# A four-stage transformer block: who splits weights, copies rows and writes results in its two expert loops

## The chip, the cores and the metric

One core of one Trainium2 chip runs the whole program. The metric is the device time of one execution in microseconds; the median of 3 runs of the kernel before is 1306.93 us (1305.28 to 1307.9).

## The reference, cut to what matters

Four stages on x of shape (4, 512, 256), each with a layer norm in front and a gated residual behind: a local AFT attention with its feed-forward, a mixture of experts (8 experts, 2 chosen for each token, squared relu, 256 hidden columns) beside a shared feed-forward, a slot attention with a GRU (3 iterations), and a second mixture of experts (8 experts, 2 chosen, silu gate, 512 hidden columns, biases).

```
x = x + tanh(g_xattn[0]) * L0_xattn(layernorm(x), ctx)
x = x + tanh(g_ffn[0])   * L0_ffn(layernorm(x))      # first expert loop, m = 0
x = x + tanh(g_xattn[1]) * L1_xattn(layernorm(x), ctx)
x = x + tanh(g_ffn[1])   * L1_ffn(layernorm(x))      # second expert loop, m = 1
# L0_ffn:  y = square(relu(x @ w1[e].T)) @ w2[e].T   for the two experts e of a token, weighted
# L1_ffn:  y = (silu(x @ gate[e] + b) * (x @ up[e] + c)) @ down[e] + d
```

## The kernel before

The kernel is written by hand for the five sequencers (TensorE, VectorE, ScalarE, GpSimd, and SP, which only issues DMAs); each works off its own program in order and waits on semaphores. Batches n = 0..3 go in two pairs (h = 0, 1). Part A makes the first attention, the shared feed-forward and the routing; part C makes slot attention and the second routing. The orders of the work there are lists of stages, one for each engine. Layer norms take the reciprocal root from GpSimd (`power`, line 836), the first of them right after GpSimd's constants.

Routing scatters each normalised token, with its place of return appended as 8 columns, into the HBM array `routed[m]`, sorted by expert (`scatter`, line 843, indirect DMAs of GpSimd). A table (lines 680 to 717) tells where each group of G = 256 rows lies and which groups each expert has: here 19 groups in the first loop and 21 in the second. `fill` (line 458) writes blank rows behind the last row of each expert: three of the fills go before the first group is fetched, five behind the first two.

The expert loops (`moe_sp`, `moe_pool`, `moe_act`, `moe_dve`, `moe_pe`) run for both m. The outer loop over experts is unrolled, the inner one over an expert's groups has its bounds from the table (`bounds`, lines 399 and 400, two register loads for each engine and expert). All products are made in three parts from a high (float32r) and a low part (the rest) of each operand: `product`, lines 210 to 212. A group t goes like this:

- SP fetches the rows of group t + 2 into `xg` (line 451, after TensorE has turned the rows of the group before) and their places into `places` (line 452).
- TensorE makes the up products of group t, then transposes the rows of group t + 1 (line 640), then waits for y of the group before and for the low part of h (`hlo`), and makes the down products into PS[5] and PS[6].
- ScalarE: relu (562), square into the high part of h (564), for each of the two blocks f of 128 hidden columns; then the high part of the next rows (544).
- VectorE: product for h in PSUM for each block (599), low part of h (588), low part of the next rows (581); then, when the down products are ready, for each half a: wait until the last write of this half has landed (`yout`), copy the places of this expert (620), copy y from PSUM to SBUF (622; in the second loop with the bias DB added, 624).
- GpSimd waits for each half of y and writes its 128 rows to `results[m]` at their places (535).

Weights of an expert come twice: `raw_in` (line 429) loads them as they are, from ScalarE's queue in the first loop, from SP's in the second; `weights_hi` (line 498) loads them once more with a cast DMA of GpSimd straight into the high part; `weights_lo` (line 507) subtracts on GpSimd (the very first of the second loop on VectorE). Weights of expert e + 2 are fetched during expert e. Between them ScalarE's queue also fetches the weights of part C (`attention_weights`, line 437), whose WHH has its high part by a cast DMA of GpSimd.

`y_free` (line 517) writes two blank rows into `results[m]`, so that `yout` counts have a start: for m = 0 after the last scatter, for m = 1 after the first loop. DB, the bias rows of the second loop's down product spread over 128 partitions (1 MB), is loaded by SP before the second routing ends (line 792).

## Time and profile before

| | us |
|---|---|
| median of 3 runs | 1306.93 |
| the profiled execution | 1311.5, its span 1309.7 |
| TensorE busy in the span | 1122.4 (86%) |
| VectorE, ScalarE, GpSimd busy | 738.5, 384.2, 375.3 |
| first expert loop, from the first up products to the last down products | 353.93 to 477.62 (start of the last product) |
| second expert loop, from the first up products to the first half of the last y | 1071.15 to 1281.2 |

The profile is of one execution. A row of its timeline has the start and the length of an instruction (of several in a row, where it ends with x2 and more), the engine, the line of the kernel, what is written and read, and in brackets how long the engine had been idle before it and what released it. "q" behind an engine is its sequencer, where DMAs are issued and registers are loaded. Matmuls overlap: a 128x256 product is listed with 0.28 us, and a new one starts every 0.12 us at the full clock of TensorE and every 0.21 us at half of it.

### The profile page before, as it was taken

What the parts mean: (1) busy time and instruction counts of PE and PEld (TensorE: products, weight loads), DVE (VectorE), ACT (ScalarE), POOL (GpSimd) and SP (SyncE); (2) the same over time, 40 slices, a digit from 0 to 9 for tenths busy, and PEclk for the clock granted to TensorE, in tenths of its full rate; (3) what the DMA queues carried; (4) which work ended last, traced back from release to release, by engine and by line L of the source; (5) the groups of instructions that cost most, each with busy time, mean ns of one, the idle gap of its engine ahead of it and who ended that gap; (6) DMA issues with size and microseconds to landing.
All of it is one profiled execution on the core that took longest, in us unless ns stands there. A gap on an engine that the chain in (4) does not pass through costs nothing.

```text
span 1309.7 us, 17730 instructions
## 1 busy us (share of the span) xinstructions
PE 1122.4 (86%) x5875; PEld 884.8 (68%) x5875; DVE 738.5 (56%) x1888; ACT 384.2 (29%) x705; POOL 375.3 (29%) x312
## 2 busy tenths in 40 slices
PE   7999899898767577899999977999999749999991
PEld 5568575685656454676887835787878439998990
DVE  5576736767344435555655554445453746666664
ACT  3131230313133224234243333243332123333330
POOL 2423161322444540001111133010101464544710
PEclk8999999999898878999999989999999969999996
DMA  9001060000566643000000000000000586555416
GB/s 324 1 0 33 3 202 8 1 1 17 160 189 181 207 127 105 22 1 1 1 1 2 1 33 34 1 1 1 1 1 1 162 259 204 153 148 169 129 56 209
DMA packets 90852, 102.93 MB, mean 79 GB/s; under 512 B 18336, under 2 KB 75936, under 8 KB 90656
## 3 DMA queue, kind: packets, MB, share of 16 engines
q1 hardware_dynamic: 65920, 59.85, 15.1%
q0 software_dynamic: 20240, 36.72, 9.1%
q10 hardware_dynamic: 4624, 5.51, 1.2%
q8 instruction: 37, 0.61, 0.2%
q14 instruction: 31, 0.25, 0.1%
HBM read 73.31 MB, written 28.74 MB: 78 GB/s over the span
## 4 chain that ended last, share of the span: by engine, by line
PE 47%; DVE 16%; another core or an unknown queue 11%; issue 7%; DMA 6%; ACT 5%; POOL 4%; SPq 3%; DVEq 1%; POOLq 0%; ACTq 0%
PE PS L210 11%; PE PS L212 10%; PE PS L211 10%; PE PS L1710 6%; PE PS L1600 2%; POOL routed L843 2%; PE PS L1572 2%; DMA results<-y,place_of 2%; POOL rstd L836 1%; DMA split<-down_w 1%; DVE SM L1397 1%; DVE hs L588 1%; PE PS L1628 1%; DMA places<-routed 1%
## 5 line engine op out<-in xcount | busy, mean ns | idle before, releaser
L836 POOL TENSOR_TENSOR rstd<-ve,minus_half 128x4 f32<-128x4 f32 x40 | 40.5, 1013 | 359.9 <-DVE ve L1099 215.0
L535 POOL DMA_INDIRECT results<-y,place_of x80 | 78.2, 978 | 186.6 <-DVE y L624 110.4
L1484 PE MATMUL PS<-ones_bf 128*128 128x512 bf16 x393 | 105.8, 417 | 16.6 <-DMA routed<-S,dest 13.5
L210 PE MATMUL PS<-xt,split 128*128 128x256 f32 x312 | 90.8, 291 | 9.3 <-issue 6.2
L1710 PE MATMUL PS<-VP,HB 128*128 128x257 f32 x384 | 85.8, 382 | 4.4 <-DVE VP L1410 4.4
L211 PE MATMUL PS<-xt,split 128*128 128x256 f32 x312 | 89.5, 287 | 0.0
L212 PE MATMUL PS<-xt,split 128*128 128x256 f32 x312 | 89.4, 287 | 0.0
L1484 PEld LDWEIGHTS PS<-ones_bf 128*128 128x128 bf16 x393 | 39.7, 107 | 70.4 <-issue 39.4
L843 POOL DMA_INDIRECT routed<-S,dest x64 | 66.8, 1044 | 67.0 <-DVE dest L1179 49.5
L1710 PEld LDWEIGHTS PS<-VP,HB 128*128 128x128 f32 x384 | 72.5, 190 | 17.4 <-DVE VP L1410 7.3
L210 PE MATMUL PS<-split,hs 128*128 128x256 f32 x184 | 59.5, 324 | 24.1 <-DVE hs L588 23.2
L567 ACT ACTIVATE act<-PS,colv 128x256 f32<-128x256 f32 x84 | 39.8, 474 | 121.9 <-PE PS L212 114.1
L210 PEld LDWEIGHTS PS<-xt,split 128*128 128x128 f32 x312 | 61.2, 196 | 11.6 <-issue 8.0
L603 DVE SCALAR_TENSOR_TENSOR act<-PS,colv,act 128x256 f32<-128x256 f32 x84 | 40.6, 484 | 37.8 <-ACT act L567 29.6
L210 PE MATMUL PS<-HTS,WHH 128*128 128x512 f32 x144 | 60.5, 420 | 1.5 <-DVE RT L1115 1.5
L211 PEld LDWEIGHTS PS<-xt,split 128*128 128x128 f32 x312 | 61.2, 196 | 0.0
L212 PEld LDWEIGHTS PS<-xt,split 128*128 128x128 f32 x312 | 61.1, 196 | 0.0
L1039 ACT ACTIVATE HB<-PS,SM 128x512 f32<-128x512 f32 x48 | 33.0, 687 | 94.0 <-DVE SM L1399 93.6
L1572 PE MATMUL PS<-EWT,HB 128*128 128x512 f32 x128 | 57.4, 608 | 3.0 <-DVE EWT L1238 3.0
L210 PEld LDWEIGHTS PS<-split,hs 128*128 128x128 f32 x184 | 36.6, 199 | 32.4 <-issue 25.8
L210 PE MATMUL PS<-RT,WIH 128*128 128x512 f32 x144 | 57.2, 397 | 0.0
L212 PE MATMUL PS<-RT,WIH 128*128 128x512 f32 x144 | 56.9, 395 | 0.0
(339 smaller groups left out, 2970.7 us busy)
## 6 DMA issues: line engine op xcount, KB each, us to landing
xg<-routed SPq DMA_DIRECT2D x42, 256.0 KB
HB<-results SPq DMA_DIRECT2D x16, 512.0 KB, 5.8
routed<-blank SPq DMA_DIRECT2D x20, 264.0 KB, 6.8
raw<-gate_w SPq DMA_DIRECT2D x8, 512.0 KB
raw<-up_w SPq DMA_DIRECT2D x8, 512.0 KB
raw<-down_w SPq DMA_DIRECT2D x8, 512.0 KB
split<-m_w POOLq DMA_DIRECT2D x12, 256.0 KB, 3.3
split<-gate_w POOLq DMA_DIRECT2D x6, 512.0 KB
```

The source lines that it names most:

```text
L210: pe.matmul(out_, a[1], b[0], start=first, stop=False)
L211: pe.matmul(out_, a[0], b[1], start=False, stop=False)
L212: return pe.matmul(out_, a[0], b[0], start=False, stop=last)
L535: pool.indirect_dma_start(out=results[m], out_offset=bass.IndirectOffsetOnAxis(ap=place_of[:, a:a + 1], axis=0), in_=w.y[:, a], in_offset= ...
L567: act.activation(w.act[:, f % 2, 0], PS[:, f, 0:G], ACT.Sigmoid, bias=col("gate_b", b)).then_inc(sem(f"m{m}_act"), 1)
L603: dve.scalar_tensor_tensor(out=a[:, 1], in0=PS[:, f, 0:G], scalar=col("gate_b", e * w.fc + f), in1=a[:, 0], op0=ALU.add, op1=ALU.mult).the ...
L836: pool.tensor_tensor(rstd[h][:], ve[h][:], minus_half[:], ALU.pow).then_inc(sem("rstd_ready"), 1)
L843: pool.indirect_dma_start(out=routed[m], out_offset=bass.IndirectOffsetOnAxis(ap=dest[m][:, n, j, kk:kk + 1], axis=0), in_=S2T[h][:, j], i ...
L1039: act.activation(HB[h][:, j], bank(h, j), ACT.Exp, bias=SM[h][:, 1, j:j + 1], scale=1.0 / 16, accum_out=SM[h][:, 2, j:j + 1]).then_inc(sem ...
L1484: pe.matmul(free.rearrange("p (a b) -> p a b", b=P), ones_bf[:], ones_bf[:].unsqueeze(1).to_broadcast([P, TT, P]), start=True, stop=True)
L1572: ins = pe.matmul(bank(h, b + c), w[:, j, c * P:(c + 1) * P], EWT[:, j], start=j == 0, stop=j == TT - 1)
L1710: ins = pe.matmul(bank(h, j)[:, 0:D + 1], HB[h][:, m, j * P:(j + 1) * P], VP[h][:, m, 0:D + 1], start=m == 0, stop=m == TT - 1)
```

## The change

- y of the first loop is copied by one instruction of ScalarE for both halves, behind the high part of the next rows; VectorE only copies the places, one instruction for both halves. There are two buffers of y and of places, for even and odd groups, and VectorE waits for the landing of the group before the last.
- GpSimd's loop for m = 0 has no experts and no weights any more: it takes two groups in a body, one with each buffer, and a last group behind. The high parts of the weights of the first loop are made by ScalarE (experts 2 to 7) and the low parts by VectorE, at the start of the expert before; on the first pair GpSimd copies the high parts of experts 0 and 1 instead of loading them. In the second loop ScalarE makes the high parts of experts 0 and 1, the others stay cast DMAs.
- The places travel with the rows: `group_in` fetches all 264 columns with one DMA, `xg` is a piece of the buffer S2T[0], and VectorE copies the 8 columns into `tags` (`tag`) between its last product and its first low part, after TensorE has turned them. SP fetches the next rows after `tagged`, not after `turned`. SP's loop has no experts either; before its third group it waits for all fills.
- `raw_in` of the second loop moves from SP's queue to ScalarE's, the two loads of X move from SP at expert 5 to ScalarE at expert 7, and the high part of WHH is made by ScalarE after the first loop.
- `y_free` for both loops moves to the start of GpSimd's program, ahead of its first `power`; for m = 0 the second half has three DMAs, and the second and third wait for the landing of the one before.
- DB is loaded after `first_group_in(sp, 1)`; VectorE waits for it (`cw_raw`, 96) after the first `x_lo` of the second loop.

```diff
-        places = sb("places", [P, (NG + 2) * (G // P), E])
-        place_of = sb("place_of", [P, G // P], I32)
+        tags = sb("tags", [P, 2, G // P, E])
+        place_of = sb("place_of", [P, 2, G // P], I32)
...
-            w.xg = sb(f"xg{m}", [P, G // P, D], F32, st)
+            w.xg = S2T[0][:, 0:G // P]
             w.xt = sb(f"xt{m}", [P, 2, C, G], F32R, st)
             w.act = sb(f"act{m}", [P, 2, w.ups, G], F32, st)
             w.hs = sb(f"hs{m}", [P, 2, w.fc, G], F32R, st)
-            w.y = sb(f"y{m}", [P, G // P, D], F32, st)
+            w.y = S1[1][:].rearrange("p (i a) d -> p i a d", i=2)
...
-        first_rows = S1[0][:, 0:G // P]
+        first_rows = S2T[0][:, G // P:2 * (G // P)]
         def group_in(sp, m, t):
             r = sp.value_load(table[m][0:1, bass.ds(t + 2 * E, 1)], min_val=0, max_val=XROWS - G)
             if not isinstance(t, int):
                 counted(sp, m)
-                sp.wait_ge(sem(f"m{m}_turned"), t)
-            into, name = (first_rows, "first_rows") if isinstance(t, int) and t == 0 else (moe[m].xg[:], f"m{m}_xg")
-            sp.dma_start(into, routed[m][bass.ds(r, G), 0:D].rearrange("(a p) d -> p a d", p=P)).then_inc(sem(name), 16)
-            sp.dma_start(places[:, bass.ds(t * (G // P), G // P)], routed[m][bass.ds(r, G), D:D + E].rearrange("(a p) e -> p a e", p=P))\
-              .then_inc(sem(f"m{m}_places"), 16)
+                sp.wait_ge(sem(f"m{m}_tagged"), t)
+            into, name = (first_rows, "first_rows") if isinstance(t, int) and t == 0 else (moe[m].xg, f"m{m}_xg")
+            sp.dma_start(into, routed[m][bass.ds(r, G), :].rearrange("(a p) d -> p a d", p=P)).then_inc(sem(name), 16)
...
+        def all_groups(eng, m):
+            return eng.value_load(table[m][0:1, 2 * E - 1:2 * E], min_val=E, max_val=NG)
         def moe_sp(sp, m):
-            for e in range(E):
-                if e == 1:
-                    sp.wait_ge(sem("filled"), 16 * (4 + (m + 1) * (E - 3)))
-                if m == 1 and e + 2 < E:
-                    raw_in(sp, m, e + 2)
-                if m == 0 and e == 5:
-                    for n, h in of_pair[0]:
-                        sp.wait_ge(sem(f"x_out{h}"), 16 * PAIRS)
-                        sp.dma_start(X[h][:], x_base[0, n].rearrange("(j p) d -> p j d", p=P)).then_inc(sem(f"x_in{h}"), 16)
-                lo, hi = bounds(sp, m, e)
-                with sp.Fori(lo, hi) as t:
-                    group_in(sp, m, t + 2)
-            moe_end(sp, m, hi)
-        def weights_hi(pool, m, e):
-            w = moe[m]
+            sp.wait_ge(sem("filled"), 16 * (4 + (m + 1) * (E - 3)))
+            total = all_groups(sp, m)
+            with sp.Fori(2, total + 1) as t:
+                group_in(sp, m, t)
+            moe_end(sp, m, total)
...
+        def weights_cast(pool, e):
+            w = moe[1]
             if e >= 3:
-                done = pool.value_load(table[m][0:1, e - 2:e - 1], min_val=1, max_val=NG - 1)
-                counted(pool, m)
-                pool.wait_ge(sem(f"m{m}_down"), done)
-            for ap, at, n in expert_sources(m, e):
-                pool.dma_start(w.split[e % 3][0][:, at:at + n].rearrange("p (c o) -> p c o", c=ap.shape[1]), ap).then_inc(sem(f"m{m}_hi{e % 2}"), 16)
+                done = pool.value_load(table[1][0:1, e - 2:e - 1], min_val=1, max_val=NG - 1)
+                counted(pool, 1)
+                pool.wait_ge(sem("m1_down"), done)
+            for ap, at, n in expert_sources(1, e):
+                pool.dma_start(w.split[e % 3][0][:, at:at + n].rearrange("p (c o) -> p c o", c=ap.shape[1]), ap).then_inc(sem(f"m1_cast{e % 2}"), 16)
+        def raw_there(eng, m, e):
+            eng.wait_ge(sem(f"m{m}_raw{e % 2}"), 16 * (m + 2) * (e // 2 + 1))
+        def weights_hi(eng, m, e):
+            raw_there(eng, m, e)
+            hi = moe[m].split[e % 3][0]
+            if eng is nc.scalar:
+                eng.activation(hi, raw_of(m, e), ACT.Copy).then_inc(sem(f"m{m}_hi"), 1)
+            else:
+                eng.tensor_copy(hi, raw_of(m, e)).then_inc(sem(f"m{m}_hi"), 1)
         def weights_lo(eng, m, e):
-            w = moe[m]
-            k = len(list(expert_sources(m, e)))
-            eng.wait_ge(sem(f"m{m}_hi{e % 2}"), 16 * k * (e // 2 + 1))
-            eng.wait_ge(sem(f"m{m}_raw{e % 2}"), 16 * k * (e // 2 + 1))
-            hi, lo = w.split[e % 3]
+            raw_there(eng, m, e)
+            if m == 0 or e < 2:
+                eng.wait_ge(sem(f"m{m}_hi"), e + 1)
+            else:
+                eng.wait_ge(sem(f"m1_cast{e % 2}"), 16 * 3 * (e // 2))
+            hi, lo = moe[m].split[e % 3]
             eng.tensor_tensor(lo, raw_of(m, e), hi.bitcast(F32), ALU.subtract).then_inc(sem(f"m{m}_lo"), 1)
...
         def y_free(pool, m):
             for a in range(G // P):
-                pool.dma_start(results[m][2 * B * T + a:2 * B * T + a + 1], blank[0:1, a, 0:D]).then_inc(sem(f"m{m}_yout{a}"), 16)
-        def moe_pool(pool, m):
-            w = moe[m]
-            pool.wait_ge(sem(f"m{m}_table"), 1)
+                for k in range(1 if m else 1 + 2 * a):
+                    if k:
+                        pool.wait_ge(sem(f"m{m}_yout{a}"), 16 * k)
+                    pool.dma_start(results[m][2 * B * T + 2 * k + a:2 * B * T + 2 * k + a + 1], blank[0:1, a, 0:D]).then_inc(sem(f"m{m}_yout{a}"), 16)
+        def rows_out(pool, m, i, a, name):
+            pool.indirect_dma_start(out=results[m], out_offset=bass.IndirectOffsetOnAxis(ap=place_of[:, i, a:a + 1], axis=0),
+                                    in_=moe[m].y[:, i, a], in_offset=None).then_inc(sem(name), 16)
+        def moe_pool_first(pool):
+            pool.wait_ge(sem("m0_table"), 1)
+            total = all_groups(pool, 0)
+            def group_out(t, i):
+                counted(pool, 0)
+                pool.wait_ge(sem("m0_y"), t + 2)
+                pool.sem_inc(sem("passed"), 1)
+                for a in range(G // P):
+                    rows_out(pool, 0, i, a, f"m0_yout{i}")
+            with pool.Fori(0, total // 2) as k:
+                for i in two:
+                    group_out(2 * k + i, i)
+            group_out(total - 1, 0)
+            moe_end(pool, 0, total)
...
-                if m == 0 and e + 2 < E:
-                    raw_in(act, 0, e + 2)
+                if e + 2 < E:
+                    raw_in(act, m, e + 2)
                 if m == 0 and 2 <= e < 7:
                     attention_weights(act, e - 2)
+                elif m == 0 and e == 7:
+                    for n, h in of_pair[0]:
+                        act.dma_start(X[h][:], x_base[0, n].rearrange("(j p) d -> p j d", p=P)).then_inc(sem(f"x_in{h}"), 16)
+                if m == 0 and 2 <= e + 1 < E:
+                    weights_hi(act, 0, e + 1)
...
                         h_hi(t, w.fc - 1)
+                    else:
+                        act.wait_ge(sem("m0_placed"), t + 1)
+                        act.wait_ge(sem("m0_down"), t + 1)
+                        act.activation(w.y[:, bass.ds(t % 2, 1)].rearrange("p i a d -> p (i a) d"), PS[:, 5:7, 0:D], ACT.Copy).then_inc(sem("m0_y"), 1)
             if m == 0:
                 moe_end(act, m, hi)
         def moe_dve(dve, m):
             w = moe[m]
+            def tag(n):
+                dve.wait_ge(sem(f"m{m}_turned"), n)
+                rows = first_rows if isinstance(n, int) else w.xg
+                dve.tensor_copy(tags[:, bass.ds((n - 1) % 2, 1)], rows[:, :, D:D + E].unsqueeze(1)).then_inc(sem(f"m{m}_tagged"), 1)
             def x_lo(n):
                 dve.wait_ge(sem(f"m{m}_xhi"), n)
...
+            tag(1)
             x_lo(1)
+            if m == 1:
+                dve.wait_ge(sem("cw_raw"), 96)
             for e in range(E):
+                if m == 0 and 2 <= e + 1 < E:
+                    weights_lo(dve, 0, e + 1)
...
+                        if f == w.fc - 1:
+                            tag(t + 2)
...
-                    dve.wait_ge(sem(f"m{m}_down"), t + 1)
-                    dve.wait_ge(sem(f"m{m}_places"), 16 * t + 16)
-                    for a in range(G // P):
-                        dve.wait_ge(sem(f"m{m}_yout{a}"), 16 * t + 16)
-                        dve.tensor_copy(place_of[:, a:a + 1], places[:, bass.ds(t * (G // P) + a, 1), e])
-                        if m == 0:
-                            dve.tensor_copy(w.y[:, a], PS[:, 5 + a, 0:D]).then_inc(sem(f"m{m}_y"), 1)
-                        else:
-                            dve.tensor_tensor(w.y[:, a], PS[:, 5 + a, 0:D], DB[:, e], ALU.add).then_inc(sem(f"m{m}_y"), 1)
+                    if m == 0:
+                        dve.wait_ge(sem("m0_yout0"), 32 * (t // 2) + 16)
+                        dve.wait_ge(sem("m0_yout1"), 32 * ((t + 1) // 2) + 16)
+                        dve.tensor_copy(place_of[:, bass.ds(t % 2, 1)], tags[:, bass.ds(t % 2, 1), :, e]).then_inc(sem("m0_placed"), 1)
+                    else:
+                        dve.wait_ge(sem("m1_down"), t + 1)
+                        for a in range(G // P):
+                            dve.wait_ge(sem(f"m1_yout{a}"), 16 * t + 16)
+                            dve.tensor_copy(place_of[:, 0, a:a + 1], tags[:, bass.ds(t % 2, 1), a, e])
+                            dve.tensor_tensor(w.y[:, 0, a], PS[:, 5 + a, 0:D], DB[:, e], ALU.add).then_inc(sem("m1_y"), 1)
...
-            sp.dma_start(DB[:], down_b.rearrange("e d -> (e d)").partition_broadcast(P).rearrange("p (e d) -> p e d", d=D)).then_inc(sem("db_in"), 16)
             first_group_in(sp, 1)
+            sp.dma_start(DB[:], down_b.rearrange("e d -> (e d)").partition_broadcast(P).rearrange("p (e d) -> p e d", d=D)).then_inc(sem("cw_raw"), 16)
...
+            pool.wait_ge(sem("blank"), 2)
+            for m in two:
+                y_free(pool, m)
...
-            pool.wait_ge(sem("blank"), 2)
-            y_free(pool, 0)
             pool.wait_ge(sem("batch_a"), B)
-            moe_pool(pool, 0)
-            y_free(pool, 1)
-            pool.wait_ge(sem("cw_hi"), 16)
+            moe_pool_first(pool)
+            pool.wait_ge(sem("cw_hi"), 1)
...
-                    if n == B - 1:
-                        pool.wait_ge(sem("batch_c"), B)
-                        for e in range(2):
-                            weights_hi(pool, 1, e)
...
+            act.wait_ge(sem("cw_raw"), 80)
+            act.activation(WHH[:, 0], raw_whh, ACT.Copy).then_inc(sem("cw_hi"), 1)
...
+            for e in range(2):
+                weights_hi(act, 1, e)
...
-            dve.wait_ge(sem("db_in"), 16)
```

## Rows read from the trace of the kernel before

**Rows 1.** One row for each stretch: us, busy us (count) of PE, PEld, DVE, ACT, POOL
```profile
353.00:479.00 126.00, 81.44 (x532) 75.75 (x532) 56.87 (x170) 38.24 (x96) 57.92 (x53) 0.87 0.63 181
...
1066.00:1290.00 224.00, 205.29 (x1608) 194.17 (x1606) 140.67 (x358) 78.86 (x192) 100.03 (x67) 0.98 0.50 148
```

**Rows 2.** Timeline, one group of the first loop: ScalarE, VectorE, TensorE
```profile
381.49 0.36 ACT L562 ACTIVATE act<-PS 128x256 f32<-128x256 f32 x1
...
382.81 0.74 DVE L588 TENSOR_TENSOR hs<-PS,hs 128x256 fp32r<-128x256 f32 x2
...
383.37 0.36 PE L210 MATMUL PS<-split,hs 128*128 128x256 f32 x1 [1.51 <-DVE hs L588]
```

**Rows 3.** Timeline, TensorE, first down product of a later group
```profile
420.79 0.36 PE L210 MATMUL PS<-split,hs 128*128 128x256 f32 x1 [0.92 <-DVE hs L588]
```

**Rows 4.** Timeline, TensorE and VectorE where the expert changes
```profile
384.76 0.28 PE L212 MATMUL PS<-split,hs 128*128 128x256 f32 x1
...
388.04 0.15 DVE L620 CAST place_of<-places 128x1 int32 x1 [1.17 <-DMA results<-y,place_of]
...
388.11 0.41 DVE L622 COPY y<-PS 128x256 f32<-128x256 f32 x1
...
389.69 0.43 DVE L599 SCALAR_TENSOR_TENSOR PS<-PS,act 128x256 f32<-128x256 f32 x1 [1.16 <-issue]
...
390.92 0.55 PE L210 MATMUL PS<-RT,hs 128*128 128x256 f32 x1 [3.25 <-DVE hs L588]
```

**Rows 5.** Timeline, TensorE, the longest wait at a change of expert
```profile
443.38 0.55 PE L210 MATMUL PS<-RT,hs 128*128 128x256 f32 x1 [5.21 <-DVE hs L588]
```

**Rows 6.** Timeline, ScalarE's DMA issues, and two instructions on 128x1024 of other stages
```profile
382.13 0.41 ACTq L429 DMA_DIRECT2D raw<-m_w  x1
...
383.16 0.61 ACTq L437 DMA_DIRECT2D HB<-Wv  x1
...
1033.04 1.02 ACT L936 ACTIVATE RT<-PS 128x1024 fp32r<-128x1024 f32 x1 [0.60 <-PE PS L1478]
...
11.52 1.23 DVE L1193 TENSOR_TENSOR EMB<-EMB,S 128x1024 f32<-128x1024 f32 x1
```

**Rows 7.** Timeline, TensorE, the rows of the third group and the down products behind
```profile
366.35 1.12 PE L640 MATMUL PS<-ident,xg 128*128 128x128 f32 x4 [4.64 <-DMA xg<-routed]
...
367.12 0.56 PE L210 MATMUL PS<-split,hs 128*128 128x256 f32 x1
```

**Rows 8.** Timeline, GpSimd at the start; line 517; issues to landing; chain; line 535
```profile
2.76 0.29 POOL L826 TENSOR_SCALAR_AFFINE_SELECT tri<-ones_bf 128x128 bf16<-128x128 bf16 x1
...
9.03 1.04 POOL L836 TENSOR_TENSOR rstd<-ve,minus_half 128x4 f32<-128x4 f32 x1 [5.97 <-DVE ve L1099]
...
L517 POOL DMA_DIRECT2D results<-blank x4: 520/540/560, 341.8 to 484.3; - x4
...
results<-blank POOLq DMA_DIRECT2D x2, 1.0 KB, 5.8
...
420.66 3.44 DMA places<-routed
...
DMA to landing us min/median/max: 2.4/2.4/4.3
```

**Rows 9.** Timeline, SP and VectorE at the second loop; issues to landing at the start
```profile
1035.25 2.79 SPq L792 DMA_DIRECT2D DB<-down_b  x1
...
1069.63 5.70 SPq L458 DMA_DIRECT2D routed<-blank  x5
...
1073.41 0.49 DVE L603 SCALAR_TENSOR_TENSOR act<-PS,colv,act 128x256 f32<-128x256 f32 x1 [2.31 <-ACT act L567]
...
band<-pos_bias SPq DMA_DIRECT2D x1, 1024.0 KB, 8.4
...
W<-w SPq DMA_DIRECT2D x1, 1024.0 KB, 11.3
```

**Rows 10.** Timeline, GpSimd's next instruction behind the first pair's weights
```profile
235.79 1.04 POOL L836 TENSOR_TENSOR rstd<-ve,minus_half 128x4 f32<-128x4 f32 x1 [32.96 <-DVE ve L1099]
```

38 lines of the change are left out of this document (17 added, 21 removed).

## The prediction

> **What bounds the kernel now.** The program is one TensorE stream with a few places where TensorE waits for others, so I read by stretch and not by share of the whole span. First the stretches of the two expert loops: in the first TensorE is busy 81 of 126 us, in the second 205 of 224 [rows 1]. So the second loop is TensorE's own, and whatever delays its first group is paid in full; the first loop loses 45 us to waits. Then the timeline of one group in the first loop, to see which wait it is. The reader is to see the chain: relu of the second hidden block on ScalarE at 381.49, VectorE's low part of the first block at 382.81, the down products at 383.37 after a wait of 1.51 us [rows 2]. VectorE's two product instructions and, ahead of them, its copies of y are what lies between. Where those copies are early, the same wait is 0.92 us [rows 3]. Last, the group at which the expert changes: VectorE stands still until the results' write has landed, then copies y at 388.11, then loads the loop bounds and restarts at 389.69, and the down products wait 3.25 us [rows 4]. There are seven such changes. Their waits are 1.51, 3.25, 3.58, 3.55, 5.21, 4.35 and 1.87 us, 23.3 us together (the second in [rows 4], the longest in [rows 5]). Of the ten other groups from the fourth on, two wait 1.5 to 1.6 us and eight 0.7 to 1.1 us (one of each in [rows 2, 3]).
>
> **First loop, inside an expert.** Removed from VectorE: two y copies of 0.41 us and two index copies of 0.15 us [rows 4]. They are on the path in two groups: 1.2 us gained (1.51 less 0.92, twice). Added: the tag copy, small like an index copy, between the second product and the first low part, where every group has it; its issue hides under the product, so I take 0.1 us, 1.1 us for eleven groups. If it hid nothing it would be 0.15 us, if all, 0. The y copy goes to ScalarE as one 128x512 instruction between the down products and the next relu. The next relu has to wait for the new group's first up products anyway, six of the twelve, which are nearly as long as the copy, so I take 0.1 us a group, 1.1 us; with no overlap it would be 0.6 us a group, with a full one 0. What is late next is again the relu, square, relu chain. ScalarE's wait for `down` queues its own relu behind it, and nobody else's work.
>
> **First loop, the change of expert.** Removed: the wait for the landed write (two buffers now), GpSimd's cast DMAs and its subtraction. Added on ScalarE, behind the last y copy: two or three DMA issues of 0.4 to 0.6 us, then the high part of 128x1024, 1.02 us like its equal [rows 6]. Added on VectorE: the low part, 1.23 us like its equal [rows 6], which waits for ScalarE, and behind which the bounds and the first product are queued. From the last down product (end 385.04, [rows 4]): y copy issued +0.3; three DMA issues, 1.65, +1.95; high part done +3.0; VectorE starts the low part, and with bounds loaded during it (388.11 to 389.69, 1.58 us, is that load beside a copy, [rows 4]) the first product starts +4.6, the second +4.95, tag, low part of h +5.35, down products +5.9. TensorE has ended its transposes at +2.6 (390.92 less 3.25, less 385.04). So the wait is 3.3 us in the five changes with a third DMA, 2.7 in the first, and about 2.5 in the last, which has no weights but two loads of X: 21.7 us for 23.3. The long waits for a landed write go, and ScalarE's and VectorE's new work takes their place: 1.6 us gained. Bounds: if none of the new work were on the path, all seven would be like the two short ones (1.7 us), 11 us gained; if the high part and the bounds of ScalarE lay one behind the other, 5 us lost.
>
> **First loop, third group.** Its rows keep TensorE waiting for 4.64 us, until 366.35 [rows 7]. SP fetched them late, after five fills and two writes of x_base. SP now waits for all fills before that fetch, and has two transfers and one bounds load fewer: about even, within 1.5 us either way. The down products of the second group, which started at 367.12, halfway through the transposes [rows 7], now wait for the end of these (367.47), the tag and the low part behind it: 368.2, 1.1 us lost. Sum of the loop: -1.2 + 1.1 + 1.1 - 1.6 + 1.1 = +0.5 us, from -12 to +6.
>
> **Start of the kernel.** `y_free` is moved ahead of GpSimd's first `power`, with six DMAs for four, and between three of them it waits for the landing. GpSimd is free at 3.05 and its `power` starts at 9.03, released by VectorE; VectorE, TensorE and all else of the first pair wait for it [rows 8]. Each issue is 0.54 us [rows 8]. With L the time from issue to landing, GpSimd is free at 3.05 + 0.54 + 2L + 3 x 0.54 = 5.2 + 2L. Two rows bound L: the same one-row DMA, sent while the other queues were filling the engines, took 5.8 us, and a small transfer amid weight loads 3.44 us [rows 8]. Here all 16 engines are loading inputs, so I take the middle, 4.6: free at 14.4, and the kernel is 5.4 us late from its first layer norm on. Nothing absorbs it: inputs are there by then. Ends: L of 2.4, the shortest landing of the indirect writes [rows 8], gives +1.0; 5.8 gives +7.8.
> The Trainium skill (DMA: Bandwidth & Descriptors, Anatomy of one DMA) fits a DMA from GpSimd as 2.0 us plus its bytes; by that alone this edit would cost 0.2 us, 5 less than my sum. It also says that an engine goes round its queues in turn. The 5.8 us for one row [rows 8] speak against taking the fit for a loaded machine, so I stay with the rows.
>
> **Start of the second loop.** DB, 1 MB, was loaded at 1035.25; its issue alone takes 2.79 us. It now goes behind the eight fills and two row fetches. The five late fills start at 1069.63 and take 5.70 us [rows 9]; two place transfers fewer make that 1.2 us earlier, so DB's issue starts at about 1074.2. Transfers of the same size in a loaded stretch land 8.4 to 11.3 us after issue [rows 9]; weights and fills load this stretch as well. I take 8.4: 1082.6. VectorE waits for it after its first x_lo, and the bounds and all products of group 0 are queued behind: 1.3 us more, 1083.9 where it was 1073.41 [rows 9]. TensorE, with the up products done, waits for the low parts. VectorE's work per block is its pace before, so the delay reaches the down products whole: +10.5 us, and [rows 1] leave no slack to win it back. Ends: landing 5 us after issue (its own issue and the shortest landing), +7.1; 11.3 us, +13.4. The cover that this load had was the whole routing of the last batches; it is gone.
>
> **What costs nothing.** On the first pair GpSimd makes the high parts by copying instead of cast DMAs, up to 1.3 us later at the second; it then stands idle 33 us [rows 10]. High part of WHH on ScalarE: 1.5 us by the 1.02 for 1024 columns [rows 6], under the eight transposes that TensorE does there; without them it would cost that. High parts of the second loop's first two experts on ScalarE fall where it idles before the table; the raw loads issued by ScalarE in the second loop lie in its wait for the up products. X is fetched 30 us later than before, still a whole expert before use. Writing results from two buffers ends as before, two issues and a landing after the last y.
>
> **Sum.** 0.5 + 5.4 + 10.5 = +16.4 us on the profiled execution's 1311.5 us (span 1309.7), which itself is 4.6 above the median 1306.93. The differences are carried over to the median: 1323.
>
> **Rivals.** (a) Faster: the boundary work of ScalarE and VectorE overlaps fully and TensorE, waiting less, also keeps its full clock; the loop gains 12 us from the waits and some 8 from clock. With head +1.0 and DB +7.1 that is 1295. For it: waits of 5.21 and 4.35 us do vanish [rows 5]. Against: the low part needs the high part, and that needs ScalarE's turn. Chance 0.11. (b) Even: the loop gains 12, the head costs 1 and DB 10.5: 1306.5, within noise. Chance 0.07. (c) Slower still, by one mechanism: at each change of expert ScalarE's DMA issues, high part and bounds load go one after another and TensorE idles beyond 4 us, falling to half clock for the next group; six times 2 us, decisive once the wait passes that of [rows 4]: 1323 + 12 = 1335. Chance 0.16. (d) The forecast, both waits real: 1323, 1312 to 1332. Chance 0.66.
>
> **How the numbers follow.** A difference of 0.2%, 2.6 us, is what a measurement of this kernel can tell from none. Faster: (a), 0.11, and a hundredth of (d). Same: (b), 0.07. Slower: the rest, 0.81. The range goes from 1307, above (a) and most of (b), to 1335, the place of (c).
>
> **What would show it.** GpSimd's first power at about 14.4 with landings of results<-blank before it; in the second loop VectorE's first product at about 1084 plus the shift, waiting for DB, and TensorE idle 8 us or more before its first down products. In the first loop: waits of 2.5 to 3.3 us at all changes, none above 4, ended by VectorE, and VectorE's low part released by ScalarE. I am wrong if DB lands before VectorE has made x_lo, if the power starts before 10, or if the stretch of the first loop, 126 us in [rows 1], is not within 114 to 132.

## The result, and the profile of the changed kernel

| | before | after |
|---|---|---|
| median of the runs, us | 1307.41 (1305.28 to 1313.71, 4 runs) | 1364.47 (1362.91 to 1365.28, 4 runs) |
| profiled execution, us (its span) | 1311.5 (1309.7) | 1362.91 (1361.2) |
| mean granted clock of TensorE | 0.947 | 0.934 |

The change makes the kernel 4.3% slower: ratio 1.0433, interval 1.0407 to 1.0459, 57 us where 16 were forecast. The spans of the two profiled executions differ by 51.5 us only: that of before took 4.1 us more than its median, that of the change 1.6 less. Read from TensorE's instructions in both traces:

| stretch of TensorE | before, us | after, us | difference |
|---|---|---|---|
| start to the first up products of the first loop | 353.93 | 363.82 | +9.9 |
| to the last down products of the first loop | 122.3 | 116.4 | -6.0 |
| to the first up products of the second loop | 594.9 | 592.0 | -2.9 |
| to its first down products | 6.2 | 18.9 | +12.7 |
| to its last down products | 199.4 | 237.9 | +38.5 |

The busy time of each engine in the two loops (columns: the stretch and its length, then busy us and instructions of TensorE, its weight loads, VectorE, ScalarE, GpSimd, then granted clock, DMA share, GB/s), to be read against [rows 1]:

```profile
363.00:486.00 123.00, 81.78 (x532) 75.19 (x532) 51.34 (x140) 55.36 (x121) 36.65 (x38) 0.87 0.49 151
1072.00:1342.00 270.00, 214.47 (x1596) 206.34 (x1596) 167.62 (x379) 78.59 (x191) 94.18 (x65) 0.90 0.39 121
```

In the second loop TensorE is busy 9 us more than in [rows 1], at a clock of 0.90 for 0.98, and idle 37 us more. VectorE is busy 27 us more, with work that hardly changed: that is the first sign, for an instruction's time as the profile counts it includes the time in which it is held up. The costliest forms of VectorE's copies of the tags show which instruction it is (count, busy us, mean ns, idle time before it), and the line's own view its spread (shortest, median, longest, ns):

```profile
L618 DVE COPY tags<-S 128x16 f32 x40 | 34.1, 852 | 1.7 <-issue 1.7
L618 DVE COPY tags<-S x42: 163/166/6435, 362.5 to 1330.2; 128x16 f32 x40, 128x16 f32<-128x16 f32 x2
```

The median is 0.166 us and the longest 6.4 us. The timelines of VectorE, GpSimd and TensorE at the third group (start us, us, engine, line, operation; the time idle before it and its releaser in brackets):

```profile
1114.11 6.43 DVE L618 COPY tags<-S 128x16 f32 x1
1120.46 0.41 DVE L629 TENSOR_TENSOR hs<-PS,hs 128x256 fp32r<-128x256 f32 x1
...
1113.78 6.73 POOL L517 TENSOR_TENSOR third_split<-raw,third_split 128x3072 fp32r<-128x3072 f32 x1
...
1120.92 0.58 PE L210 MATMUL PS<-split,hs 128*128 128x256 f32 x1 [6.42 <-DVE hs L629]
```

GpSimd's subtraction starts at 1113.78 and ends at 1120.51; VectorE's copy of 16 columns starts a third of a us later and ends at 1120.54. The low part of h stands behind it, and TensorE stops in the midst of its down products for 6.42 us and comes back slower (0.58 us, then 0.41 to 0.42 each, for instructions that took 0.28 before the stop). It happens six times: at 1114.11, 1152.67, 1188.09, 1234.22, 1260.34 and 1286.84, with copies of 6.43, 4.58, 4.66, 4.68, 4.63 and 2.44 us. The six sets of down products take 10.6, 8.8, 8.9, 8.9, 8.9 and 6.3 us where the others take 3.4: 32 of the 38.5 us. Cut the other way, from the first down products to the last, TensorE is idle for 34.8 us where before has 7.5, and busy for 203.1 where before has 191.9, at a granted clock of 0.93 for 1.00: 27 us more of waiting and 11 us more of running at the lower clock after the stops.

The start of the kernel, GpSimd and below it VectorE, against [rows 8]:

```profile
3.37 1.25 POOL L525 DMA_DIRECT2D results<-blank  x2 [0.31 <-POOL tri L875]
9.79 0.48 POOL L525 DMA_DIRECT2D results<-blank  x1 [5.18 <-DMA results<-blank]
14.66 1.43 POOL L525 DMA_DIRECT2D results<-blank  x3 [4.39 <-DMA results<-blank]
16.11 1.07 POOL L888 TENSOR_TENSOR rstd<-ve,minus_half 128x4 f32<-128x4 f32 x1
17.14 1.93 POOL L901 TENSOR_SCALAR_AFFINE_SELECT band<-band 128x2048 f32<-128x2048 f32 x1
...
17.22 4.63 DVE L1159 TENSOR_SCALAR EMB<-X,mv,rstd 128x256 f32<-128x256 f32 x4 [8.81 <-POOL rstd L888]
```

The two waits for landings put `power` at 16.11, 7.1 us late, and VectorE's scaling, released by it, then runs beside GpSimd's two selects on `band` (the position bias, of which they keep a band) and takes 4.63 us where before it took 1.38. Together that is the 10 us of the table.

The start of the second loop, on SP, on the chain of waits (start us, us, what) and on VectorE, against [rows 9]:

```profile
1068.79 6.09 SPq L457 DMA_DIRECT2D routed<-blank  x5
1074.91 0.47 SPq L842 DMA_DIRECT2D DB<-down_b  x1
...
1074.91 12.29 DMA DB<-down_b
1087.24 0.32 DVEq L399
...
1088.71 0.48 DVE L649 SCALAR_TENSOR_TENSOR act<-PS,colv,act 128x256 f32<-128x256 f32 x1 [16.63 <-issue]
```

DB lands 12.29 us after its issue; bounds (L399, L400) and the first product stand behind the wait, and the first down products start at 1091.01 after 11.10 us of idle TensorE.

The first loop, at the second change of expert, on ScalarE, VectorE and TensorE, against [rows 4] and [rows 6]:

```profile
396.99 0.60 ACT L608 ACTIVATE S<-PS 128x512 f32 x1 [1.90 <-PE PS L212]
397.15 0.90 ACTq L429 DMA_DIRECT2D raw<-m_w  x2
398.14 0.43 ACTq L437 DMA_DIRECT2D HB<-Wv  x1
398.62 1.06 ACT L505 ACTIVATE split<-S 128x1024 fp32r<-128x1024 f32 x1 [1.03 <-issue]
...
399.78 1.22 DVE L517 TENSOR_TENSOR split<-S,split 128x1024 fp32r<-128x1024 f32 x1 [3.68 <-ACT split L505]
401.23 0.77 DVE L645 SCALAR_TENSOR_TENSOR PS<-PS,act 128x256 f32<-128x256 f32 x2 [0.23 <-issue]
...
402.45 0.38 PE L210 MATMUL PS<-RT,hs 128*128 128x256 f32 x1 [3.16 <-DVE hs L629]
```

That is the forecast chain: ScalarE's y copy, its three issues, the high part, VectorE's low part and products, the down products. The waits at the seven changes are 3.85, 3.16, 3.17, 3.02, 3.59, 2.09 and 2.14 us, 21.0 together.

### The profile page after: what moved, and what is told of

Same layout as the page of the kernel before. It is cut to its first block, busy times and chain, and to the rows that moved or that the text cites. A ratio compares the mean times of both kernels' runs of the same rounds, so it can differ in the third digit from the quotient of the medians.

```text
span 1361.2 us, 17338 instructions
## 1 busy us (share of the span) xinstructions
PE 1127.6 (83%) x5875; PEld 893.9 (66%) x5875; DVE 763.4 (56%) x1879; ACT 408.6 (30%) x733; POOL 345.3 (25%) x287
## 3 DMA queue, kind: packets, MB, share of 16 engines
q1 hardware_dynamic: 45920, 48.82, 11.3%
## 4 chain that ended last, share of the span: by engine, by line
PE 48%; DVE 17%; another core or an unknown queue 11%; issue 8%; ACT 5%; POOL 4%; DMA 3%; SPq 1%; ACTq 1%; DVEq 1%; POOLq 0%
PE PS L210 12%; PE PS L212 11%; PE PS L211 10%; PE PS L1757 6%; POOL routed L895 2%; PE PS L1647 2%; PE PS L1619 2%; POOL rstd L888 1%; DVE hs L629 1%; DVE SM L1445 1%; DVE act L649 1%; PE PS L1525 1%; ACT HB L1085 1%; DMA DB<-down_b 1%
## 5 line engine op out<-in xcount | busy, mean ns | idle before, releaser
L528 POOL DMA_INDIRECT results<-S,place_of x80 | 77.7, 971 | 267.8 <-DVE S L673 154.7
L210 PE MATMUL PS<-split,hs 128*128 128x256 f32 x184 | 62.5, 340 | 53.1 <-DVE hs L629 50.0
L210 PE MATMUL PS<-xt,split 128*128 128x256 f32 x312 | 93.7, 300 | 8.9 <-issue 5.9
L211 PE MATMUL PS<-xt,split 128*128 128x256 f32 x312 | 91.9, 295 | 0.0
L212 PE MATMUL PS<-xt,split 128*128 128x256 f32 x312 | 91.6, 294 | 0.0
L210 PEld LDWEIGHTS PS<-xt,split 128*128 128x128 f32 x312 | 64.2, 206 | 11.7 <-issue 7.9
L211 PEld LDWEIGHTS PS<-xt,split 128*128 128x128 f32 x312 | 64.2, 206 | 0.0
L212 PEld LDWEIGHTS PS<-xt,split 128*128 128x128 f32 x312 | 63.6, 204 | 0.0
```

Of the source, the lines that this page charges most:

```text
L210: pe.matmul(out_, a[1], b[0], start=first, stop=False)
L211: pe.matmul(out_, a[0], b[1], start=False, stop=False)
L212: return pe.matmul(out_, a[0], b[0], start=False, stop=last)
L528: pool.indirect_dma_start(out=results[m], out_offset=bass.IndirectOffsetOnAxis(ap=place_of[:, i, a:a + 1], axis=0), in_=moe[m].y[:, i, a], ...
```

## The experiments

Two theories at the outset. **Lock**: GpSimd and VectorE share a way to SBUF that one instruction holds to its end, and a VectorE copy or scaling from SBUF to SBUF needs it. **Rival**: the long copies wait for something of their own (the row that they read, their data type, descriptor writing by GpSimd's queue). Beside them stand DB's place in SP's queue and `y_free`'s place in GpSimd's as causes of their own. Each time is given as the ratio to the kernel before, measured beside it; a difference to the changed kernel is that of the two ratios times 1307. It carries about 4 to 6 us of uncertainty, an estimate from the 95% intervals of the ratios. In the expectations e1 is kernel 1 below, and so on.

**1. The tag copy on ScalarE.** Behind `x_hi`, in both loops; VectorE waits for it only ahead of the place copy. In the second loop ScalarE first waits for y of the group before.

```diff
                     x_hi(t + 2)
                     if m == 1:
+                        act.wait_ge(sem("m1_y"), 2 * t + 1)
+                    tag(t + 2)
+                    if m == 1:
                         h_hi(t, w.fc - 1)
...
-                        if f == w.fc - 1:
-                            tag(t + 2)
...
+                    dve.wait_ge(sem(f"m{m}_tagged"), t + 1)
```

> The changed kernel with the tag copy on ScalarE in both loops (behind the high part of the next rows) and VectorE waiting for it only before it copies the places. In the changed kernel six tag copies of the second loop, beside GpSimd's subtraction of weights, last 2.8 to 6.4 us instead of 0.17 us, and the low part of h is queued behind them. Theory P (the copy from SBUF to SBUF and GpSimd's subtraction cannot run at once): no long tag copy is left, because ScalarE does not share with GpSimd; all down products of the second loop from its second group on take 3.4 us; 1364 minus 32 to 38 us, so 1326 to 1332. Rival W (what is late there are the weights or rows, because the loads moved from SP's queue to ScalarE's, and the copy only shows it): the down products of those six groups stay 5 to 7 us too long and the time stays within 4 us of 1364.

Measured: 1330.9 us, ratio 1.0179 (1.0156 to 1.0203), 33 us less than the change. GpSimd, ScalarE, and the first and the last of TensorE's down products of one group:

```profile
1141.14 6.88 POOL L517 TENSOR_TENSOR split<-raw,split 128x3072 fp32r<-128x3072 f32 x1
...
1142.96 0.23 ACT L575 ACTIVATE tags<-S 128x16 f32 x1
...
1142.00 0.36 PE L210 MATMUL PS<-third_split,hs 128*128 128x256 f32 x1
...
1145.37 0.28 PE L212 MATMUL PS<-third_split,hs 128*128 128x256 f32 x1
```

The subtraction still takes 6.9 us, ScalarE's copy in the midst of it 0.23, and the down products are back at 3.4. VectorE's products and low parts, of which at least one input lies in PSUM, run through beside the subtraction at their usual 0.41 to 0.49 us. That rules out late weights or rows, the rival in the expectation. The tag copy carries the greater part of the loss; the run doesn't say yet what holds it.

**2. DB ahead of the fills again.**

```diff
+            sp.dma_start(DB[:], down_b...).then_inc(sem("cw_raw"), 16)
             first_group_in(sp, 1)
-            sp.dma_start(DB[:], down_b...).then_inc(sem("cw_raw"), 16)
```

> The changed kernel with the load of DB back ahead of first_group_in of the second loop. Theory D (VectorE waits for DB, which lands 12.3 us after its issue at 1074.91): VectorE's first product of the second loop starts about 1.5 us after x_lo as before, TensorE does not wait 11.1 us ahead of its first down products; 12 to 14 us less, so 1350 to 1352. If the first group is late for another reason (fills, rows, table load of ScalarE), the time stays within 3 us of 1364 and that wait stays above 8 us.

Measured: 1352.93 us, ratio 1.0338 (1.0318 to 1.0358), 12.4 us less than the change by the ratios and 11.5 by the medians. DB's issue stands at 1043.03, and TensorE's first down products at 1083.56 directly behind the transposes, with no wait. The term is real: TensorE's wait of 11.10 us, and 1.6 us by which the first two sets of down products are longer behind it (4.9 and 3.4 us from first to last start, here 3.9 and 2.8).

**3. `y_free` behind the second `power`.**

```diff
-            pool.wait_ge(sem("blank"), 2)
-            for m in two:
-                y_free(pool, m)
...
             power(1)
+            pool.wait_ge(sem("blank"), 2)
+            for m in two:
+                y_free(pool, m)
```

> The changed kernel with both y_free behind GpSimd's second power, where it is idle for some 20 us. Theory Y (the two waits for a landing, 5.2 us each, hold GpSimd's first power, and the band selection behind it holds VectorE's scaling, 4.63 us instead of 1.38 us): the first power is at about 9.0 us, VectorE's scaling takes 1.4 us, its second statistics are at 17.0 us instead of 27.4; 10 us less, so 1353 to 1356. If the band load or another input were the bound anyway, VectorE's second statistics would stay behind 20 us and no more than 4 us would come back.

Measured: 1354.69 us, ratio 1.0371 (1.0337 to 1.0404), 8.1 us less by the ratios, 9.8 by the medians; the first up products stand at 354.26 for 363.82. `power` is back at 8.56 and, what matters for experiment 6, the band select now comes after the scaling:

```profile
8.56 1.04 POOL L885 TENSOR_TENSOR rstd<-ve,minus_half 128x4 f32<-128x4 f32 x1 [5.51 <-DVE ve L1147]
14.35 1.92 POOL L898 TENSOR_SCALAR_AFFINE_SELECT band<-band 128x2048 f32<-128x2048 f32 x1 [4.74 <-DMA band<-pos_bias]
...
9.64 1.38 DVE L1159 TENSOR_SCALAR EMB<-X,mv,rstd 128x256 f32<-128x256 f32 x4 [1.23 <-POOL rstd L885]
```

The select waits for its own load until 14.35; only because `y_free` pushed `power` beyond that do the two meet.

**4. GpSimd's subtraction in two halves.**

```diff
+            if m == 1 and e >= 2:
+                k = moe[m].cols // 2
+                eng.tensor_tensor(lo[:, 0:k], raw_of(m, e)[:, 0:k], hi[:, 0:k].bitcast(F32), ALU.subtract)
+                eng.tensor_tensor(lo[:, k:], raw_of(m, e)[:, k:], hi[:, k:].bitcast(F32), ALU.subtract)...
```

> The changed kernel with GpSimd's subtraction for experts 1 to 7 of the second loop made as two instructions on 1536 columns each instead of one on 3072 (from expert 2 on). Theory P with a lock held for one whole instruction: the tag copy waits only for the rest of the first half; the six long copies (about 5 us each) shrink to 1.5 to 3.4 us or vanish, and 12 to 25 us come back: 1340 to 1352. If VectorE had to wait until GpSimd has nothing queued that reads SBUF, the copies stay as long and so does the time, within 3 us of 1364. Rival W: no change either, but then the copies' length has no relation to the end of a half.

Measured: 1366.97 us, ratio 1.0455 (1.043 to 1.048): no gain. GpSimd and VectorE:

```profile
1115.96 3.49 POOL L519 TENSOR_TENSOR third_split<-raw,third_split 128x1536 fp32r<-128x1536 f32 x1
1119.37 3.46 POOL L520 TENSOR_TENSOR third_split<-raw,third_split 128x1536 fp32r<-128x1536 f32 x1
...
1116.29 6.58 DVE L623 COPY tags<-S 128x16 f32 x1
```

The copy waits through both halves. The second half begins (1119.37) before the record of the first ends (1119.45), and VectorE isn't let in between. All six long copies are like that. But two GpSimd instructions in line don't always count as one. At the start of the changed kernel GpSimd's second select waits by semaphore for its first, and there VectorE's first two scalings end one behind each select (GpSimd's second select; VectorE's first and second scaling):

```profile
19.14 1.92 POOL L904 TENSOR_SCALAR_AFFINE_SELECT band<-band 128x2048 f32<-128x2048 f32 x1
...
17.22 2.02 DVE L1159 TENSOR_SCALAR EMB<-X,mv,rstd 128x256 f32<-128x256 f32 x1 [8.81 <-POOL rstd L888]
...
19.15 2.05 DVE L1159 TENSOR_SCALAR EMB<-X,mv,rstd 128x256 f32<-128x256 f32 x1
```

The first select ends at 19.07, the first scaling at 19.24. So VectorE waits as long as GpSimd's instructions stand back to back, and got its turn where GpSimd had waited in between. Halves with a wait between them weren't tried.

**5. Tags as integers.** The copy becomes a cast from fp32 to int32 of the same 128x16.

```diff
-        tags = sb("tags", [P, 2, G // P, E])
+        tags = sb("tags", [P, 2, G // P, E], I32)
```

> The changed kernel with the tags kept as int32, so that VectorE's tag copy turns float32 into int32 on its way; engine, place and size (128x16) stay. What is open: whether the form of the instruction or only its source in SBUF makes it wait for GpSimd. In the kernel before, VectorE's cast of 128x1 from SBUF ran in 0.15 us while GpSimd's subtraction ran. Theory F (only the plain copy has to wait): no long tag copy, 32 to 38 us less than 1364, 1326 to 1332. Theory S (a wide enough read from SBUF waits in either form): the six long copies and 1364 stay.

Measured: 1367.6 us, ratio 1.046 (1.0443 to 1.0476). The cast waits like the copy:

```profile
1116.90 6.46 DVE L618 CAST tags<-S 128x16 f32 x1
...
1116.59 6.73 POOL L517 TENSOR_TENSOR third_split<-raw,third_split 128x3072 fp32r<-128x3072 f32 x1
```

So the form of the output isn't it. One form is exempt, though, and it is the one from which I had priced the tag copy. In the kernel before, ten place copies of 128x1 fall inside GpSimd's subtractions, and none takes over 0.15 us (GpSimd, then VectorE, of before):

```profile
1097.05 6.88 POOL L507 TENSOR_TENSOR third_split<-raw,third_split 128x3072 fp32r<-128x3072 f32 x1
...
1102.39 0.15 DVE L620 CAST place_of<-places 128x1 int32 x1 [1.77 <-DMA places<-routed]
```

Experiment 1 has the same: casts of 128x1 inside the subtractions take 0.15 us. 128x1 isn't held and 128x16 is, as copy and as cast. Where between them the border lies, and whether it is the count of columns or the layout, wasn't tried.

**6. The band select behind the first scaling.** GpSimd's select waits until VectorE has finished its first embedding.

```diff
             pool.wait_ge(sem("pb_in"), 16)
+            pool.wait_ge(sem("emb"), 1)
```

> The changed kernel, y_free in front as it is, but GpSimd's selection on the band waits until VectorE has made the first EMB. Theory: of the 10 us at the start, 3.2 us are VectorE's scaling (SBUF to SBUF, 4.63 us for 1.38 us) standing still while GpSimd selects; with the hold it takes 1.4 us, nothing waits for the band, and 3 us come back: about 1361. If the scaling is slow for the DMA traffic, it stays at 4.6 us and so does the time.

Measured: 1364.15 us, ratio 1.0439 (1.0423 to 1.0454): no gain in the total. In the trace the mechanism is there (VectorE, then GpSimd):

```profile
17.30 1.38 DVE L1160 TENSOR_SCALAR EMB<-X,mv,rstd 128x256 f32<-128x256 f32 x4 [8.63 <-POOL rstd L888]
...
19.86 1.75 DVE L1248 TENSOR_TENSOR W<-HB,W 128x1536 fp32r<-128x1536 f32 x1
...
20.08 3.31 POOL L902 TENSOR_SCALAR_AFFINE_SELECT band<-band 128x2048 f32<-128x2048 f32 x1 [2.81 <-DVE EMB L1242]
```

The scaling is back at 1.38 us, and now it is GpSimd that waits: its select takes 3.31 us, because it starts inside VectorE's subtraction with two SBUF inputs (19.86 to 21.61). The lock works both ways. VectorE's maximum over the band comes 3.3 us earlier (35.37 for 38.67) and the first up products 2.0 us (361.85 for 363.82). Then it is lost by steps: the third group's rows are waited for 3.25 us where it was 1.69, the last down products of the first loop come 0.7 us earlier, the first of the second 0.1 us. Between kernels with the same code up to there the place of the first up products varies by more than that: it is 363.8 to 365.1 in the changed kernel and experiments 1, 2, 4 and 5, which all keep this start, and 357.85 in experiment 10, which keeps it too. What 3 us at the head are worth at the end I can't tell from this run.

**7. The three repairs together**: the edits of 1, 2 and 3 in one kernel, ScalarE's copy with its wait, DB first, `y_free` last.

> The tag copy on ScalarE, DB early and y_free late, all three. If the parts add up: 1364.5 - 33.6 - 11.5 - 9.8 = 1309.6. By the stages of the traces the first loop and the way into slot attention are 6 and 3 us shorter than before, which would make it 1299 to 1303 where before is 1308. I expect 1300 to 1309; above 1312 a further loss would be open.

Measured: 1304.15 us (11 runs), ratio 0.9969 (0.9953 to 0.9985). The three take 60.6 us by the ratios, 7 more than the 33, 12.4 and 8.1 that they took alone, which is within what the intervals of the five ratios allow together (about 9 us, an estimate): they account for the whole loss of 57 and leave a small gain, 4 us. By the stretches of the table above against before: start 0.0, first loop -5.8, the middle -3.2, first group of the second loop 0.0, its rest +0.9 us. So the change does what it was made for: the first loop is 6 us shorter. The stretches together say 8 us, twice the gain of the ratio, because the profiled execution of before is 4 us above its median; which stretch holds these 4 us isn't known.

**8. The high part ahead of ScalarE's DMA issues**, on top of 7.

```diff
             for e in range(E):
+                if m == 0 and 2 <= e + 1 < E:
+                    weights_hi(act, 0, e + 1)
                 if e + 2 < E:
                     raw_in(act, m, e + 2)
...
-                if m == 0 and 2 <= e + 1 < E:
-                    weights_hi(act, 0, e + 1)
```

> As e7_three, and in the first loop ScalarE makes the high part of the next expert's weights ahead of its DMA issues, not behind. Theory: at a change of expert TensorE waits 3.0 to 3.9 us for the chain y copy, DMA issues (0.9 to 1.6 us), high part, low part, products; without the issues in it the six waits fall to 1.7 to 2.5 us: 6 to 9 us less than e7_three. If instead VectorE's loop bounds set the restart, less than 2 us come back.

Measured: 1301.16 us, ratio 0.9955 (0.9939 to 0.9971). ScalarE at the second change of expert:

```profile
383.68 0.60 ACT L616 ACTIVATE S<-PS 128x512 f32 x1 [1.35 <-PE PS L212]
383.87 0.38 ACTq L429 DMA_DIRECT2D raw<-m_w  x1
384.17 1.05 ACT L505 ACTIVATE split<-S 128x1024 fp32r<-128x1024 f32 x1
...
386.84 0.38 ACT L599 ACTIVATE act<-PS 128x256 f32<-128x256 f32 x1 [1.61 <-issue]
```

The high part follows the y copy at once, the issues run during it. Of the seven waits six are 2.3 to 2.5 us and one 1.7: 16.0 us, where 7 has 20.3. The gain, 2 to 4 us, is less than expected. In the chain of waits ScalarE's own bounds load (L399, L400), 385.32 to 386.32, stands behind its issues, and with it the next relu at 386.84 (the 1.61 us by "issue"); VectorE's low part, 1.23 us from 385.33, runs beside the load and is done before the relu starts.

**9. VectorE's first subtraction behind GpSimd's scatter**, on top of 8. The kernel before has the same meeting the other way round: an issue of a scatter that takes 3.69 us (its neighbours 0.96) beside VectorE's subtraction of two SBUF inputs. From the trace of before, GpSimd and VectorE:

```profile
1057.27 3.69 POOL L843 DMA_INDIRECT routed<-S,dest  x1 [0.30 <-issue]
...
1056.78 3.34 DVE L507 TENSOR_TENSOR split<-raw,split 128x3072 fp32r<-128x3072 f32 x1
```

```diff
+            pool.sem_inc(sem("pool_c"), 1)
...
+            dve.wait_ge(sem("pool_c"), 18)
             weights_lo(dve, 1, 0)
```

> The kernel of e8 with one wait more: VectorE's subtraction of the low part of expert 0's weights for the second loop (3.34 us in before) waits until GpSimd has issued the last indirect scatter of part C. Before, this subtraction started at 1056.78 and the scatter issue at 1057.27, which took 3.69 us where the others take about 1.0. Theory lock (GpSimd and VectorE can't use their common way to SBUF at once, whichever came first): the scatter issue falls to about 1.0 us, rows, places and the second loop's first up products come about 2.6 us earlier: 1298.5 against e8's 1301.2. Rival (the 3.69 us is the scatter's own work, or the subtraction moved behind it becomes the last thing that the first up products wait for): no change or up to 1 us slower, 1301 to 1302.

GpSimd's increment is written behind its last scatter.

Measured: 1293.46 us, ratio 0.9918 (0.9897 to 0.9939). It tells nothing about the theory, since the wait held nothing back: VectorE's subtraction starts at 1036.41 and GpSimd's last scatter issue at 1044.70, and the scatter beside it takes 3.61 us as ever. By the increments written in the program the count of 18 can't be there before GpSimd's last one, so this ran ahead of the DMA issues that stand before it. And so the ratio is one more draw of kernel 8.

**10. GpSimd's subtractions on VectorE**, tag copy where the change has it.

```diff
-                if 1 <= e < E - 1:
-                    weights_lo(pool, 1, e + 1)
...
-                if m == 0 and 2 <= e + 1 < E:
-                    weights_lo(dve, 0, e + 1)
+                if 2 - m <= e + 1 < E:
+                    weights_lo(dve, m, e + 1)
```

> The changed kernel with GpSimd's seven subtractions of the second loop (6.7 us each) on VectorE (3.34 us each, ahead of the expert's groups); the tag copy stays on VectorE, GpSimd keeps its casting DMAs and indirect scatters. Theory lock with the subtraction: no tag copy above 0.2 us is left, the down products are back at 3.4 us, -32 to -35 us; against that stand seven subtractions of 3.34 us in VectorE's queue, of which 0 to all lies on the path (0 to +23): 1330 to 1354. Rival (what holds the tag copy is GpSimd's descriptor writing for its DMAs, not the subtraction): the copies stay at 2.4 to 6.4 us and the time is 1364 or more, up to 1388.

Measured: 1326.81 us, ratio 1.0186 (1.0167 to 1.0204), 32 us less than the change. VectorE's copies of the tags (shortest, median, longest, ns); one of them inside the issue of a casting DMA; and one of VectorE's subtractions with the issue that GpSimd starts beside it:

```profile
L616 DVE COPY tags<-S x42: 164/166/323, 356.2 to 1288.2; 128x16 f32 x40, 128x16 f32<-128x16 f32 x2
...
1105.18 0.80 POOL L494 DMA_DIRECT2D split<-down_w  x1
...
1105.82 0.17 DVE L616 COPY tags<-S 128x16 f32 x1
...
1128.73 3.35 DVE L517 TENSOR_TENSOR split<-raw,split 128x3072 fp32r<-128x3072 f32 x1
...
1129.21 3.70 POOL L528 DMA_INDIRECT results<-S,place_of  x1 [7.45 <-DVE S L671]
```

No copy is over 0.33 us, and five of the second loop start inside the issue of a casting DMA and take 0.17. So it is the subtraction that holds the copy, not GpSimd's queue for DMAs. With 1, 4 and 5 the runs show that the two instructions exclude each other; that it is one way to SBUF which they share remains the theory's picture of it. From the second group on, every set of down products takes 3.4 to 4.0 us, and from the first down products to the last are 204.6 us where before has 199.4: of seven subtractions of 3.35 us on VectorE, 23.4 us in all, 5 are paid and the rest is hidden.

The last two lines show the other direction. GpSimd's issue of an indirect DMA takes 0.96 us by itself. Here it takes 3.70 and ends at 1132.91, 0.83 us after VectorE's subtraction. This is the rule in every trace of this case: of the 87 indirect issues that start inside a VectorE subtraction of two SBUF inputs of 128x1024 or 128x3072, 86 end 0.82 to 0.85 us after it and one 0.94, whenever they began. In this kernel they are eleven, in the kernel before three (at 769.04, 795.90 and 1057.27).

**11. The subtraction of 9 behind the landing of the scattered rows**, on top of 8.

```diff
+            for h in two:
+                dve.wait_ge(sem(f"scattered{h}"), 16 * 2 * TT * PAIRS * 2)
             weights_lo(dve, 1, 0)
```

> In e9 the added wait held nothing back: its trace has VectorE's subtraction at 1036.41 while GpSimd's last scatter issue starts at 1044.70, and the scatter issue at 1036.98 took 3.61 us (GpSimd's semaphore increment ran ahead of the issues queued before it). Here the subtraction waits for the landing of all scattered rows instead. Theory lock: all 16 scatter issues take about 1.0 us, the last one and all that follows come 2.6 us earlier in relation to the first (21.8 us from first to last issue becomes about 19.0), the time is 2 to 3 us (0.2%) under e12, which is e8 once more. Rival (a scatter issue of 3.6 us is its own work): 21.8 us from first to last stay, the time is that of e12. Second rival: the subtraction, now behind the landing, is late for the first up products; they come no earlier and the time is that of e12 or up to 2 us over it.

Measured: 1299.48 us, ratio 0.9939 (0.9918 to 0.9959), that of kernel 12 (below) within 0.2 us. The scatter does what the lock says: none of its issues takes over 1.2 us, and from first to last start are 19.2 us (1029.49 to 1048.73), in kernel 12 22.3 (1029.20 to 1051.47, with one issue of 3.97). The 2.7 us are lost one queue further. SP in kernel 11, then in kernel 12:

```profile
1045.06 7.40 SPq L457 DMA_DIRECT2D routed<-blank  x3
...
1045.42 2.08 SPq L458 DMA_DIRECT2D routed<-blank  x3
```

The three fills, which the row fetch has to wait for, take 7.40 us to issue where they took 2.08, and the rows are fetched no earlier (1055.00, in kernel 12 1054.70). In the chain of waits SP's own instructions between the fills (L456) stand 0.7 us apart, at 1045.76, 1046.46 and 1047.16. It is the second rival's result, by another cause than it named. Why SP is slow there wasn't tried, and whether it has to do with the moved subtraction stays open.

**12. Kernel 8 once more**, beside 11.

> The same program as e8 (the three repairs, and the weights' high part ahead of ScalarE's DMA issues), once more, to stand beside e11 and to show how well such a ratio repeats: e8 gave 0.9955 and e9, which differs from it by a wait that was met at once, 0.9918. If both are draws around one value, this gives 0.993 to 0.995, 1300 us at a kernel before of 1307; a value outside 0.990 to 0.998 would say that something else changed.

Measured: 1299.64 us, ratio 0.9939 (0.9918 to 0.996). Three measurements of this kernel give 0.9955, 0.9918 and 0.9939: it is 0.4 to 0.8% faster than the kernel before, the best version found, and two such ratios may differ by 0.004 with nothing changed. The 2 to 4 us of experiment 8 over 7 are of that size.

## Why the prediction was wrong

The direction and both waits that it named were right; the size was short by 41 us. By its own steps:

- **The tag copy, "small like an index copy", 0.1 us**: the step that failed. It was priced from the 0.15 us row of a 128x1 copy, and only in the first loop; the second loop, where the new instruction of 128x16 runs beside GpSimd's 128x3072 subtraction, got no term. There it costs 33 us (experiment 1, -33; experiment 10, -32 by another way, with 5 us paid for the subtractions that moved). By the stretch of the down products in the profiles it is 38 us both ways: 237.9 us became 200.2, and 204.6 with those 5. [rows 1] had said that every delay in the second loop is paid in full. And the trace of before had a warning that I read past: the scatter issue of 3.69 us beside VectorE's subtraction. The Trainium skill (SBUF — State Buffer, Who interferes with whom) states that copies, casts and scalings in their two-port form contend with GpSimd, and that the second to issue "fully blocks". This case's trace agrees: 6.43 us for 0.166. I hadn't weighed it, though the change adds an SBUF to SBUF copy on VectorE and leaves GpSimd its subtraction.
- **Start of the kernel, +5.4**: mechanism right, power at 14.4 forecast and 16.11 measured. In the chain of waits the two landings took 5.42 and 4.59 us where 4.6 was taken; the other 0.9 us are 0.3 until GpSimd issues again behind each of them, and a start at 3.37 for 3.05. The second part was missed: late by 7 us, the scaling meets the band select and waits 3.3 us. "Nothing absorbs it" was true, but what a delay collides with has to be asked too. The trace's 9.9 us were forecast as 5.4; removed by experiment 3, 8 to 10 us.
- **Start of the second loop, +10.5**: mechanism right in every link. Issue at 1074.91 for 1074.2. The landing took 12.29 us where I took 8.4, the lower of the two rows, and beyond the upper end of 11.3; the six profiles with the load at this place and GpSimd's subtractions as in the change have 12.0 to 13.3 us, that of experiment 10 has 7.29, and why isn't known. The first down products came 13.6 us later (1077.38 to 1091.01), 1.0 of it inherited. Experiment 2: 11.5 to 12.4 us.
- **Change of expert in the first loop, -1.6**: right in mechanism and sum, 21.0 us for 21.7, with VectorE's low part released by ScalarE's high part. In part the sum is luck: the first change, forecast at 2.7 for want of a third DMA, is the longest with 3.85, and the sixth is 2.09 where 3.3 was forecast. "None above 4" holds in this profile; in those of experiments 2, 3 and 6, with the same code there, and of 7, one change has 4.2 to 4.8 us.
- **The other terms of the first loop, +2.1 together**: too high. The loop came out 6 us shorter in the profile, 5.8 in that of kernel 7. Of this 2.3 us are the changes of expert. The third group's wait fell from 4.64 to 1.69 us (3.12 in kernel 7), where "about even" was forecast; in the other groups tag and y copy cost nothing that the waits of 0.8 to 0.9 us show.
- **Rivals.** (a) named the right gain for the first loop in kind but half of it came, and it needed the head and DB to be cheap; (c) forecast waits above 4 us at each change, which aren't there. None of them was a contention between two engines.
- **The middle of the kernel, taken as even**, is 3 us shorter, in kernel 7 as well. In the changed kernel 2 us of it lie between the last down products and the products of the attention keys (27.9 us for 29.9), but not in kernel 7 (29.8); where it comes from stays open.

The sum with the measured sizes: 9.9 - 6.0 - 2.9 + 12.7 + 38.5 = +52 us on the profiles.

## What to carry to other kernels

Price a small instruction by the company it will keep: for each copy or scaling from SBUF to SBUF that a change gives to VectorE, look what GpSimd runs at that moment, and take GpSimd's longest instruction, or row of them back to back, as the upper end. Put such a copy on ScalarE, or GpSimd's long work on VectorE, rather than split it in two. A load moved behind others in a queue costs its landing under that load, so take at least the upper row; and where a delay is certain, ask what the delayed work will now run beside.
